# Tile 0 by expert id, six of W2's experts on ScalarE and VectorE, and the seam between the two layers in a new order

## The chip, the cores and the metric

The kernel runs on one core of one Trainium2 chip. The metric is device time in microseconds of one launch; the median of three runs of the kernel before is 280.23 us (279.22 to 280.51). Lower is better.

## What is computed

Eight sequences of 512 rows of 256 numbers pass two layers. The first is an attention that keeps only row sums: `q` and `k` are projections with rotary position, `o = exp(q k / 16)` summed over the causal keys, and `x1 = layernorm(x + relu(o * fc1_w + fc1_b) @ fc2_w.T + fc2_b)`. The second is a mixture of twelve experts, of which the router keeps three for each row and each of three weightings:

```python
h = gelu(sum_e C1[:, e] * (x1 @ W1[e].T))        # C1: softmax over the three largest logits, 0 elsewhere
y = sum_e C2[:, e] * (h @ W2[e].T) + C3 @ b2
out = layernorm(x1 + y)
```

The kernel reads from its own counts (`route_count`, `route_ids`, `load_ids`) which experts any row of a group of four tiles has chosen, computes three by their ids, and repeats everything with all twelve if a count shows more than three in a group; the trace has no such repeat.

## The kernel before, in words

There are 32 tiles (`NT`) of 128 rows, in eight groups of four (`GT`). Every engine runs one list of instructions in order; all waits between engines are semaphores written out by hand, so the order inside each engine's list is the schedule.

**The first layer** goes in eight chunks c = 0 to 7 (`NCH`) of four sequences each. TensorE projects four column blocks (`project(c, 0..3)`, line 920) and takes the scores of the chunk before (`scores`, line 933). ScalarE copies each projection out of PSUM (`qk_copy`, line 661) and takes the exponentials (`exps`, line 669). VectorE turns by position (`rope`, lines 1289 and 1295). Between these, `early_aux(c, j, early)` places the steps of the second layer's groups 0 and 1 by a list `EARLY` (line 340): ScalarE's `normed(0, 0)` (line 713) stands in chunk 4 ahead of `w_high(0)`, `qk_copy(4, 2)` and `exps(3, 1)`; TensorE's `x1_transpose(0, 0)` (line 1007) and `gate_spread(3)` (line 943) stand at the end of chunk 4, ahead of `project(5, 0)`. `normed(g, 0)` waits for `rstd_done`, which GpSimd's `norm_scale(g)` (lines 496 to 499) raises; that one waits for VectorE's `norm_stats(g)` (lines 1365 and 1369).

**The weights** W1 and W2 are each scaled by a power of two and split into a high and a low half in 16 bits. Experts 0 to 3 (`NB = 4`) of each go to ScalarE (`w_high`, line 699) and VectorE (`w_low`, line 1334). The other eight of each go to GpSimd (`w_piece`, three instructions: line 468 scales into `wtmp`, line 470 rounds, line 471 subtracts), one after another; the first waits for the DMAs of `fc2s`, which read from `wtmp`. GpSimd's loop (lines 567 to 586) runs `norm_scale(0)` at (3, 3), ahead of all pieces, and `norm_scale(1)` before piece 5.

**The seam** is the stretch between the last projection and the steady loop (`for i in range(GT, NT + 2)`). TensorE's list for it stands in lines 1176 to 1235, VectorE's in 1580 to 1616, ScalarE's in 846 to 871, GpSimd's in 585 to 611. Tile 0 is computed there with all twelve experts of W1 (`first`) and of W2 (`second(0, ...)`), since the ids come late; tiles 1 to 3 take three experts by id (`routed_first`, `second`). A product of a tile with an expert is six matmuls (`products`, line 1117) into one of four PSUM banks (`place`, `before`); VectorE adds most of them (`add_slot`, line 1535), ScalarE the first one of a tile (`begin`, line 783). Tile t goes through `gelu` (line 788), `h_transpose` (line 1197), `h_high` (line 830), `h_low` (line 1575), and W2's products. PSUM bank `XPOSE` is shared by `x1_transpose` (copied out by `x1_high`, line 720, and `x1_low`, line 1377), `C3_transpose` and `gate_transpose` (line 955, copied by `gate_copy`, line 690); whoever writes it waits for the readers of the one before. Bank `ROWS` is shared by `fc` (line 995, read by `fc_add`, line 1359) and `bias` (line 1059, read by `bias_copy`, line 726).

**The loop** runs from i = 4. In i = 4 ScalarE does `normed(3, 0)`, `begin_second(2)`, `h_high(3)`, `bias_copy`, `begin(4)`, `exp_route(2)` (line 705), `gelu(4)`. Exp and gelu need different tables, and a table load stands in the trace where they alternate.

Of the kernel before, what the change touches and what calls it, by code (L numbers as in the profile page):

```python
# [33 lines left out]
NB = 4  # L34
# [51 lines left out]
def build(nc, x, xT, wqkT, gate, fc2, p_w, uT, w1T, w2T, b2e, constb, constf, out):  # L86
    ctx = ExitStack()
    with ctx:
# [142 lines left out]
        w_split = sem("w_split")  # L231
        wlo_done = sem("wlo_done")
# [71 lines left out]
        def experts_of(t):  # L304
            return NE if t == 0 else TOPK

# [22 lines left out]
        def dense_expert(m, j):  # L329

            return NB - 1 - j if m and j < NB else j

        def last(t, m):
            return t, m, experts_of(t) - 1
# [24 lines left out]

        PARTS = (slice(0, NB), slice(NB + 2, NB + 6), slice(NB + 6, WS))  # L360
        HALVES = [slice(p.start + 2 * n, p.start + 2 * n + 2) for p in PARTS for n in range(2)]

# [3 lines left out]
        def _(sp):  # L366
# [12 lines left out]
            def load_experts(m, w):  # L379
                sp.dma_start(Wf[:, WS * m:WS * m + NB, :], w[:, 0:NB, :]).then_inc(ld_w[m], 16)  # L380
                sp.dma_start(Wf[:, WS * m + NB + 2:WS * (m + 1), :], w[:, NB:NE, :]).then_inc(ld_w[m], 16)

# [48 lines left out]
        def _(pool):  # L431
# [101 lines left out]
            def select_of(g):  # L533
# [5 lines left out]
                t = slice(max(GT * g, 1), GT * (g + 1))  # L539
# [106 lines left out]
        def _(act):  # L646
# [47 lines left out]
            def w_high(n):  # L694
                m, e = n // NB, NB - 1 - n % NB
                act.wait_ge(scale_done, 1)
                if n % NB:
# [77 lines left out]
            def begin(t):  # L775
                n = slot[t, 0, 0]
                if t == 0:
                    act.wait_ge(C_done, 1)
                elif t % GT == 0 or t == 1:
                    act.wait_ge(csel_done, t // GT + 1)  # L780
                act.wait_ge(slot_done, n + 1)
                c0 = C[:, 0, 0, 1:2] if t == 0 else Csel[:, t, 0, 0:1]
                act.activation(acc1[:, t % 2, :], bank[place[n]][:, 0:DIM], ACT.Copy, scale=c0).then_inc(acc_begun, 1)
# [6 lines left out]
            for c in range(NCH):  # L790
# [4 lines left out]
                if c == 0:  # L795
                    act.wait_ge(ld_const, 16 * 6)
                if c:
                    exps(c - 1, 0)
                early_aux(c, 0, early)
                early_aux(c, 1, early)  # L800
                if c == 2:
                    w_sum(0)
# [5 lines left out]
                if c:  # L808
                    exps(c - 1, 1)
                if c == 2:  # L810
# [11 lines left out]
                if c == NCH - 2:  # L822
                    x1_high(1, 0)
                    w_high(NB)
                if c == NCH - 1:
                    w_high(NB + 1)
# [43 lines left out]
            begin(3)  # L870
            gelu(3)
# [41 lines left out]
        def _(pe):  # L913
# [114 lines left out]
            def route_count(g):  # L1028
# [3 lines left out]
                tiles = range(1 if g == 0 else 0, GT)  # L1032
                for t in tiles:
                    mm = pe.matmul(bank[MISC][0:1, Z:Z + NM * NE], const(C_ONES, 1),
                                   mask[:, NR * t:NR * t + NM, :].rearrange("p g e -> p (g e)"),
                                   start=(t == tiles[0]), stop=(t == GT - 1))
# [84 lines left out]
            def mixture(t, m, lhs, js):  # L1121
                for j in js:
# [4 lines left out]
                    e = dense_expert(m, j) + 1 if t == 0 else held_ids[t // GT][REC * m + j]  # L1127
                    products(bank[place[n]], lhs, m, e).then_inc(slot_done, 1)
# [13 lines left out]
            for c in range(NCH):  # L1142
# [12 lines left out]
                if c:  # L1155
                    scores(c - 1, 0)
                project(c, 2)
                early_aux(c, 2, early)
                if c == NCH - 1:
                    route_count(0)  # L1160
# [11 lines left out]

            def first(js):
                mixture(0, 0, lambda hx, c: x1T[:, 0, hx, c, :], js)

            x1_transpose(1, 1)
            pe.wait_ge(exp_done, SPC * (NCH - 1))
            pe.wait_ge(w_split, NE - NB)
            pe.wait_ge(wlo_done, NB)
            first(range(0, 2))  # L1180
            pe.wait_ge(qk_copied, 4 * NCH)
            first(range(2, 4))
            fc(2, 0)
            first(range(4, 6))
            pe.wait_ge(gate_copied, 4)
            load_ids(0)
            scores(NCH - 1, 0)
            first(range(6, 8))
            fc(2, 1)
            scores(NCH - 1, 1)  # L1190
            first(range(8, NE))
# [14 lines left out]

            C3_transpose(0)
            routed_first(1)
# [4 lines left out]
            pe.wait_ge(wlo_done, NM * NB - 1)  # L1213
            second(0, range(0, NB - 1))
            pe.wait_ge(wlo_done, NM * NB)
            second(0, range(NB - 1, NB))
            pe.wait_ge(w_split, NM * (NE - NB) - 2)
            second(0, range(NB, NB + 2))
            bias(0, 1)
            second(0, range(NB + 2, NE - 2))  # L1220
            x1_transpose(2, 0)
            pe.wait_ge(w_split, NM * (NE - NB))
            second(0, range(NE - 2, NE))
            h_transpose(1)
            routed_first(2)
            fc(3, 0)
            gate_transpose(2)
            route_count(1)
            second(1, range(0, 1))
            fc(3, 1)  # L1230
            second(1, range(1, TOPK))
            h_transpose(2)
            x1_transpose(2, 1)
            routed_first(3)
# [38 lines left out]
        def _(dve):  # L1273
# [57 lines left out]
            def w_low(n):  # L1331
                m, e = n // NB, NB - 1 - n % NB
# [63 lines left out]
            def route_strike(g, halves=(0, 1)):  # L1396
# [5 lines left out]
                for n in range(n3 // 2 * halves[0], n3 // 2 * (halves[-1] + 1)):  # L1402
                    if g == 0 or n % NR == NM:
# [4 lines left out]
            def route_mask(g):  # L1408
                wait(dve, count_done, g)
                wait(dve, ezm_done, g)  # L1410
                if g == 0:
# [343 lines left out]
```

## Time and profile before

| | |
|---|---|
| median of 3 runs | 280.23 us |
| time of the profiled execution | 280.48 us |
| its span | 278.7 us |
| TensorE busy | 257.4 us (92%) |
| VectorE, GpSimd, ScalarE busy | 213.2, 180.2, 173.9 us |
| mean granted TensorE clock | 0.98 of full |

The profiled execution is one run; its time is 1.78 us above its span. PE is TensorE, DVE is VectorE, ACT is ScalarE, POOL is GpSimd. Starts are counted from the start of the span. An "idle before" names what ended the wait. Instructions of one engine overlap a little, so the time that one takes in a queue is the distance to the next start rather than its own duration.

### The profile page before, as it was taken

How to read it: one execution, taken by the hardware profiler on the slowest of the kernel's cores; microseconds unless marked ns; L12 is line 12 of the kernel's file. 1: busy time of each engine (PE TensorE's matmuls, PEld its weight loads, DVE VectorE, ACT ScalarE, POOL GpSimd, SP SyncE). 2: the span in 40 equal slices, each digit the busy share in tenths (PEclk: the TensorE clock that was granted, in tenths of full speed). 3: DMA queues.
4: the chain of work that ended last, by engine and by line, in shares of the span. 5: the costliest groups of instructions: out<-in, count | busy, mean ns of one | idle time of the engine just before them, and what ended most of it. 6: DMA issues, size and time to landing. Idle time of an engine off the chain costs nothing.

```text
span 278.7 us, 6485 instructions
## 1 busy us (share of the span) xinstructions
PE 257.4 (92%) x2016; PEld 191.4 (69%) x2016; DVE 213.2 (77%) x668; ACT 173.9 (62%) x376; POOL 180.2 (65%) x367
## 2 busy tenths in 40 slices
PE   7999999998989985998999999999999999899980
PEld 5445444554436773877789798799798798798960
DVE  0359959859969865688998899899897788766671
ACT  2235975765852730675958957967878858656541
POOL 2640004999989899747885775775775864856551
PEclk9999999999999996899999999999999999999996
DMA  7999994996000000000010101001011010111012
GB/s 226 378 397 372 164 221 72 220 151 84 0 1 2 0 4 0 0 5 17 13 31 22 34 24 39 22 20 42 19 26 35 20 40 19 33 32 38 23 36 61
DMA packets 19546, 20.51 MB, mean 74 GB/s; under 512 B 1643, under 2 KB 18870, under 8 KB 18998
## 3 DMA queue, kind: packets, MB, share of 16 engines
q1 hardware_dynamic: 18518, 19.14, 27.9%
q10 hardware_dynamic: 992, 0.93, 1.2%
q8 instruction: 18, 0.29, 0.4%
q14 instruction: 18, 0.15, 0.2%
HBM read 15.78 MB, written 4.19 MB: 72 GB/s over the span
## 4 chain that ended last, share of the span: by engine, by line
PE 37%; POOL 21%; SPq 16%; ACT 12%; issue 6%; DVE 5%; DMA 1%; POOLq 0%; ACTq 0%; DVEq 0%
PE bank L1117 31%; POOL W L471 7%; POOL wtmp L468 5%; POOL W L470 5%; SPq L371 4%; SPq L376 3%; ACT L705 3%; SPq L393 2%; SPq L380 2%; DVE early L1535 2%; ACT early L726 2%; PE bank L1197 2%; ACT L788 2%; SPq L404 1%; PE bank L995 1%
## 5 line engine op out<-in xcount | busy, mean ns | idle before, releaser
L1117 PE MATMUL bank<-W,early 128*128 (+1 forms) x630 | 77.7, 278 | 6.0 <-DVE early L1535 3.7
L1117 PE MATMUL bank<-W,x1T 128*128 (+1 forms) x630 | 75.9, 273 | 0.5 <-ACT early L837 0.5
L1117 PEld LDWEIGHTS bank<-W,early 128*128 128x128 f16 x630 | 61.9, 100 | 15.8 <-issue 4.2
L1117 PEld LDWEIGHTS bank<-W,x1T 128*128 128x128 f16 x630 | 60.9, 98 | 8.6 <-issue 1.1
L920 PE MATMUL bank<-early,wqk 128*128 128x512 f32 x128 | 60.1, 602 | 1.1 <-DMA early<-in_xT 1.1
L1535 DVE SCALAR_TENSOR_TENSOR early<-bank,Csel,early 128x256 f32<-128x256 f32 x95 | 45.7, 481 | 9.2 <-PE bank L1117 2.7
L591 POOL TENSOR_TENSOR early<-early 128x256 f32<-128x256 f32 x29 | 21.0, 725 | 28.4 <-DVE early L1535 27.1
L920 PEld LDWEIGHTS bank<-early,wqk 128*128 128x128 f32 x128 | 22.4, 190 | 21.8 <-issue 21.2
L661 ACT ACTIVATE qk<-bank 128x512 bf16<-128x512 f32 x32 | 19.0, 595 | 29.1 <-PE bank L920 28.9
L788 ACT ACTIVATE early<-early 128x256 f32<-128x256 f32 x32 | 13.3, 417 | 35.5 <-DVE early L1535 35.4
L1289 DVE TENSOR_TENSOR xturn<-qk,turn 128x2048 bf16<-128x2048 bf16 x16 | 20.4, 1276 | 15.7 <-ACT qk L661 15.7
L713 ACT ACTIVATE x<-xs,shift,rstd 128x256 f32<-128x256 f32 x32 | 17.4, 593 | 9.4 <-POOL shift L499 9.4
L843 ACT ACTIVATE early<-early,shift,rstd 128x256 f32<-128x256 f32 x32 | 18.8, 587 | 4.5 <-POOL shift L599 4.4
L471 POOL TENSOR_TENSOR W<-wtmp,W 128x512 f16<-128x512 f32 x16 | 20.6, 1289 | 1.4
L1535 DVE SCALAR_TENSOR_TENSOR early<-bank,Csel,xs 128x256 f32<-128x256 f32 x31 | 14.7, 473 | 8.4 <-PE bank L1117 7.2
L496 POOL TENSOR_SCALAR ve<-mv 128x4 f32<-128x4 f32 x8 | 2.8, 352 | 28.0 <-DVE mv L1369 27.5
L669 ACT ACTIVATE expd<-bank 128x128 bf16<-128x128 f32 (+3 forms) x32 | 13.6, 435 | 10.9 <-PE bank L935 10.8
L504 POOL TENSOR_TENSOR xs<-early,x 128x512 f32<-128x512 f32 x16 | 20.3, 1267 | 0.0
L598 POOL TENSOR_TENSOR rstd<-ve,minus_half 128x1 f32<-128x1 f32 x32 | 18.0, 561 | 2.7
L830 ACT ACTIVATE early<-bank,ipow 128x256 f16<-128x256 f32 x32 | 14.9, 467 | 5.4 <-PE bank L1197 5.2
L1575 DVE SCALAR_TENSOR_TENSOR early<-bank,ipow,early 128x256 f16<-128x256 f32 x32 | 14.7, 460 | 3.8 <-ACT early L830 3.8
L468 POOL TENSOR_SCALAR wtmp<-W,scale 128x512 f32<-128x512 f32 x16 | 15.4, 960 | 0.9 <-DMA fc2s<-wtmp 0.9
(139 smaller groups left out, 451.6 us busy)
## 6 DMA issues: line engine op xcount, KB each, us to landing
early<-in_xT SPq DMA_DIRECT2D x16, 256.0 KB, 7.8
xs<-in_x SPq DMA_DIRECT2D x32, 128.0 KB, 6.8
out<-early SPq DMA_DIRECT2D x32, 128.0 KB
W<-in_w1T SPq DMA_DIRECT2D x1, 2048.0 KB, 12.2
W<-in_w2T SPq DMA_DIRECT2D x1, 2048.0 KB, 12.8
W<-in_w1T SPq DMA_DIRECT2D x1, 1024.0 KB, 7.7
W<-in_w2T SPq DMA_DIRECT2D x1, 1024.0 KB, 14.3
wqk<-in_wqkT ACTq DMA_DIRECT2D x1, 512.0 KB, 3.8
```

The costliest lines, as they stand in the source:

```text
L468: link(pool.tensor_scalar(wtmp[:, n % 2, :], Wf[:, WS * m + e + 2, :], scale[:, 1 + m:2 + m], 0.0, ALU.mult, ALU.add))
L471: pool.tensor_tensor(W[:, m, e + 1, 1, :], wtmp[:, n % 2, :], W[:, m, e + 1, 0, :], ALU.subtract)\
L504: pool.tensor_tensor(xs[:, t:t + 2, :].rearrange("p t d -> p (t d)"), brows[:, h, :], x1[:, g % 3, 2 * h:2 * h + 2, :].rearrange("p t d -> ...
L591: pool.tensor_tensor(y[:, t % 4, :], y[:, t % 4, :], part[:, t % 2, :], ALU.add).then_inc(late_added, 1)
L598: link(pool.tensor_tensor(rstd2[:, p:p + 1], ve2[:, p:p + 1], minus_half[:, 0:1], ALU.pow))
L661: act.activation(qk[:, c % 2, g, :, :].rearrange("p s n -> p (s n)"), bank[PROJ[n % 2]][:, :], ACT.Copy)\
L788: act.activation(hact[:, t % 2, :], acc1[:, t % 2, :], ACT.Gelu).then_inc(gelu_done, 1)
L843: act.activation(y[:, t % 4, :], y[:, t % 4, :], ACT.Identity, bias=shift2[:, p:p + 1], scale=rstd2[:, p:p + 1]).then_inc(y_done, 1)
L920: mm = pe.matmul(bank[PROJ[n % 2]][:, :], wqk[:, k, g, :], xTb[:, c % 4, k, :, :].rearrange("p s n -> p (s n)"), start=(k == 0), stop=(k = ...
L1117: mm = pe.matmul(where[:, 0:DIM], lhs(hx, c), w, start=(k == 0), stop=(k == 5))
L1289: link(dve.tensor_tensor(xturn[:, :, :, :, :], src, turns, ALU.mult))
L1535: dve.scalar_tensor_tensor(sums, bank[place[n]][:, 0:DIM], c, before, ALU.mult, ALU.add)\
```

## The change

Tile 0 takes the three experts of its group's ids, as all other tiles do, for W1 and for W2; `dense_expert` and the twelve-expert lists go. `NB` becomes a pair: four experts of W1 and six of W2 are split by ScalarE and VectorE. GpSimd's last six (of W2) are scaled in place by ScalarE (`w_pre`), and GpSimd rounds and subtracts only. `load_ids(0)` moves ahead of the seam, and the seam's lists are in a new order on all four engines: three tiles and then the fourth of W1's products come before tile 0's of W2. In chunk 7, `route_count(0)` moves ahead of `project(7, 2)`, `rope(7, 1)` is run in the loop, `w_pre(8)` to `w_pre(10)` and `w_low(4)` are added. `begin(t)` also waits for `gelu_done`. `route_mask(0)` takes the form of the other groups, with four strikes in place of twelve. The diff, cut to its core (removed lines of the seam's lists that only moved are left out with their context):

```diff
-NB = 4
+NB = (4, 6)
+HERE, THERE = NB[0], NE - NB[0]
...
-        def experts_of(t):
-            return NE if t == 0 else TOPK
...
-            order = [(i - 2, 1, j) for j in range(experts_of(i - 2))] if i >= 2 else []
-            order += [(i, 0, j) for j in range(experts_of(i))] if i < NT else []
+            seconds = () if i < GT else (0, 1, 2) if i == GT else (i - 2,)
+            order = [(t, 1, j) for t in seconds for j in range(TOPK)]
+            order += [(i, 0, j) for j in range(TOPK)] if i < NT else []
...
+        def here(n):
+            return (0, NB[0] - 1 - n) if n < HERE else (1, NB[1] - 1 - (n - HERE))
+
+        def there(n):
+            return (0, NB[0] + n) if n < THERE else (1, NB[1] + n - THERE)
...
             def w_piece(n):
-                m, e = n // (NE - NB), NB + n % (NE - NB)
+                m, e = there(n)
                 if n == 0:
                     pool.wait_ge(fc2_spread, 16 * NP)
                     pool.wait_ge(scale_done, 1)
+                if m:
+                    raw = Wf[:, WS * m + e + 2, :]
+                    pool.wait_ge(pre_done, n - THERE + 1)
+                    pool.wait_ge(w_split, n)
+                    link(pool.tensor_copy(W[:, m, e + 1, 0, :], raw))
+                    pool.tensor_tensor(W[:, m, e + 1, 1, :], raw, W[:, m, e + 1, 0, :], ALU.subtract).then_inc(w_split, 1)
+                    return
...
-            piece = 0
-            for c in range(NCH):
-                for j in range(4):
-                    if (c, j) == (NCH - 1, 1):
-                        continue
-                    if (c, j) == (3, 3):
-                        norm_scale(0)
-                    if (c, j) == (5, 1):
-                        norm_scale(1)
-                    if (c, j) == (6, 1):
-                        chosen_exps(0)
-                        weights_of(0)
-                    if (c, j) == (6, 2):
-                        C3_split(0)
-                        select_of(0)
-                    if c >= 4:
-                        w_piece(piece)
-                        piece += 1
-            bias_add(0, 0)
-            w_piece(piece)
+            for n in range(THERE):
+                if n == 3:
+                    norm_scale(0)
+                if n == 5:
+                    norm_scale(1)
+                w_piece(n)
+            chosen_exps(0)
+            weights_of(0)
+            select_of(0)
+            C3_split(0)
+            for n in range(THERE, 2 * NE - sum(NB)):
+                if n == 2 * NE - sum(NB) - 1:
+                    bias_add(0, 0)
+                w_piece(n)
...
             norm_scale(2)
+            bias_add(0, 1)
             gate_parts(2)
-            bias_add(0, 1)
+            chosen_exps(1)
             row_scale(0)
-            chosen_exps(1)
...
+            def w_pre(n):
+                m, e = there(n)
+                act.wait_ge(scale_done, 1)
+                raw = Wf[:, WS * m + e + 2, :]
+                act.activation(raw, raw, ACT.Copy, scale=scale[:, 1 + m:2 + m]).then_inc(pre_done, 1)
...
             begin(0)
+            w_pre(THERE + 3)
+            begin(1)
+            w_pre(THERE + 4)
+            w_pre(THERE + 5)
             exps(NCH - 1, 0)
-            w_high(NB + 2)
+            w_high(HERE + 2)
             exps(NCH - 1, 1)
-            w_high(NB + 3)
+            w_high(HERE + 3)
+            C3T_copy(0)
             gelu(0)
-            C3T_copy(0)
-            begin(1)
+            gelu(1)
+            begin(2)
+            w_high(HERE + 4)
+            bias_copy(0, 0)
             h_high(0)
-            bias_copy(0, 0)
-            gelu(1)
+            gelu(2)
+            w_high(HERE + 5)
+            begin(3)
+            h_high(1)
+            bias_copy(0, 1)
+            gelu(3)
             normed(2, 0)
-            bias_copy(0, 1)
+            exp_route(1)
             x1_high(2, 0)
-            exp_route(1)
             normed(2, 1)
-            h_high(1)
-            begin(2)
-            gelu(2)
-            gate_copy(2)
             final(0)
             h_high(2)
             x1_high(2, 1)
-            begin(3)
-            gelu(3)
+            gate_copy(2)
...
+            load_ids(0)
+            x1_transpose(1, 1)
+            pe.wait_ge(exp_done, SPC * (NCH - 1))
+            pe.wait_ge(w_split, THERE)
+            pe.wait_ge(wlo_done, HERE)
+            routed_first(0, range(0, 2))
+            pe.wait_ge(qk_copied, 4 * NCH)
+            routed_first(0, range(2, TOPK))
+            fc(2, 0)
+            routed_first(1, range(0, 2))
+            pe.wait_ge(gate_copied, 4)
+            scores(NCH - 1, 0)
+            routed_first(1, range(2, TOPK))
+            fc(2, 1)
+            scores(NCH - 1, 1)
             C3_transpose(0)
-            routed_first(1)
+            routed_first(2)
             pe.wait_ge(exp_done, SPC * NCH)
             h_transpose(0)
             bias(0, 0)
             route_logits(1)
...
+            h_transpose(1)
+            routed_first(3)
             bias(0, 1)
...
+            pe.wait_ge(wlo_done, sum(NB))
+            pe.wait_ge(w_split, 2 * NE - sum(NB))
+            second(0, range(TOPK))
             x1_transpose(2, 0)
...
             fc(3, 0)
...
+            second(1, range(TOPK))
             h_transpose(2)
             x1_transpose(2, 1)
-            routed_first(3)
+            route_count(1)
+            fc(3, 1)
+            gate_transpose(2)
             fc(4, 0)
...
+            first_mixture(0)
             fc_add(2, 0)
...
             x1_low(1, 1)
...
+            w_low(HERE + 1)
+            first_mixture(1)
             fc_add(2, 1)
...
+            w_low(HERE + 2)
             norm_stats(2)
...
+            w_low(HERE + 3)
+            first_mixture(2)
             h_low(0)
...
+            w_low(HERE + 4)
             route_max(1)
...
+            w_low(HERE + 5)
+            first_mixture(3)
+            h_low(1)
+            second_mixture(0)
+            x1_low(2, 0)
             route_strike(1)
...
+            route_mask(1)
             row_stats(0)
...
             fc_add(3, 0)
...
+            second_mixture(1)
             route_sums(1)
...
             row_stats(1)
             h_low(2)
             x1_low(2, 1)
...
+            route_ids(1)
+            fc_add(3, 1)
+            norm_stats(3)
             fc_add(4, 0)
```

## Rows read from the trace of the kernel before

**Rows 1.** The page: busy us, share of the span and instructions of each engine.
```profile
PE 257.4 (92%) x2016; PEld 191.4 (69%) x2016; DVE 213.2 (77%) x668; ACT 173.9 (62%) x376; POOL 180.2 (65%) x367
```

**Rows 2.** Timeline, GpSimd: start us, us, engine line operation, count, idle before.
```profile
44.30 1.12 POOL L496 TENSOR_SCALAR ve<-mv 128x4 f32<-128x4 f32 x1 [26.88 <-DVE mv L1369]
...
48.48 1.00 POOL L468 TENSOR_SCALAR wtmp<-W,scale 128x512 f32<-128x512 f32 x1 [0.91 <-DMA fc2s<-wtmp]
...
56.45 0.69 POOL L468 TENSOR_SCALAR wtmp<-W,scale 128x512 f32<-128x512 f32 x1
...
59.03 0.69 POOL L468 TENSOR_SCALAR wtmp<-W,scale 128x512 f32<-128x512 f32 x1
```

**Rows 3.** Timeline, ScalarE, in chunk 4.
```profile
47.78 1.09 ACT L713 ACTIVATE x<-xs,shift,rstd 128x256 f32<-128x256 f32 x2
...
50.21 0.40 ACT L669 ACTIVATE expd<-bank 128x256 bf16<-128x256 f32 x1
```

**Rows 4.** Timeline, TensorE, chunks 4 to 6.
```profile
51.02 0.60 PE L1007 MATMUL bank<-identf,x 128*128 128x128 f32 x4
51.46 0.60 PE L943 MATMUL bank<-identf,o 128*32 128x128 f32 x4
...
68.32 0.50 PE L933 MATMUL bank<-x1T,qr 128*128 128x384 bf16 x2 [0.83 <-DVE x1T L1295]
...
84.04 0.60 PE L1007 MATMUL bank<-identf,x 128*128 128x128 f32 x4
```

**Rows 5.** Windows: busy us of PE, PEld, DVE, ACT, POOL; granted PE clock; DMA.
```profile
106.00:107.00 1.00, 0.00 (x0) 0.00 (x0) 0.00 (x0) 0.00 (x0) 1.00 (x2) 0.98 0.00 0
107.00:108.00 1.00, 0.04 (x1) 0.07 (x2) 0.63 (x2) 0.00 (x0) 0.97 (x2) 0.50 0.00 0
...
113.00:114.00 1.00, 1.00 (x8) 0.73 (x6) 0.23 (x1) 0.50 (x2) 0.93 (x2) 0.60 0.00 0
```

**Rows 6.** Timeline, TensorE, in the seam.
```profile
97.51 2.13 PE L1117 MATMUL bank<-W,x1T 128*128 x18
...
107.96 2.72 PE L1117 MATMUL bank<-W,early 128*128 128x256 f16 x12 [3.66 <-DVE early L1535]
...
127.53 0.77 PE L1023 MATMUL bank<-MT,x1T 128*128 128x36 f16 x24 [0.29 <-DVE x1T L1377]
```

**Rows 7.** Timeline, GpSimd, in the seam.
```profile
98.63 0.61 POOL L470 CAST W<-wtmp 128x512 f16<-128x512 f32 x1
...
100.46 1.13 POOL L468 TENSOR_SCALAR wtmp<-W,scale 128x512 f32<-128x512 f32 x1
...
109.97 0.23 POOL L496 TENSOR_SCALAR ve<-mv 128x4 f32<-128x4 f32 x1
...
111.85 0.42 POOL L483 TENSOR_TENSOR hg<-o,gwb 128x136 f32<-128x136 f32 x1
...
115.68 1.27 POOL L504 TENSOR_TENSOR xs<-early,x 128x512 f32<-128x512 f32 x1
```

**Rows 8.** Timeline, VectorE, in the seam.
```profile
108.77 0.36 DVE L1385 TENSOR_SCALAR zs<-bank,iscale 128x144 f32<-128x144 f32 x1
...
110.58 1.52 DVE L1535 SCALAR_TENSOR_TENSOR early<-bank,C,early 128x256 f32<-128x256 f32 x3
...
119.58 0.68 DVE L1377 TENSOR_TENSOR x1T<-bank,x1T 128x512 f16<-128x512 f32 x1
...
128.17 0.25 DVE L1369 BATCH_NORM_AGGREGATE mv<-stats 128x2 f32<-128x6 f32 x2
```

**Rows 9.** Timeline, ScalarE, in the seam.
```profile
95.53 0.72 ACT L699 ACTIVATE W<-W,scale 128x512 f16<-128x512 f32 x1
96.27 1.28 ACT L788 ACT_TABLE_LOAD   x1
98.07 0.42 ACT L788 ACTIVATE early<-early 128x256 f32<-128x256 f32 x1 [0.52 <-DVE early L1535]
...
133.14 1.28 ACT L705 ACT_TABLE_LOAD   x1
```

More of the change, by code:

```diff
@@ L358, in later @@
             return 2 <= g < NG
-        PARTS = (slice(0, NB), slice(NB + 2, NB + 6), slice(NB + 6, WS))
-        HALVES = [slice(p.start + 2 * n, p.start + 2 * n + 2) for p in PARTS for n in range(2)]
+        PARTS = (slice(0, NB[0]), slice(NB[0] + 2, NB[0] + 6), slice(NB[0] + 6, WS))
+        HALVES = [slice(e + 2 * (e >= NB[1]), e + 2 * (e >= NB[1]) + 2) for e in range(0, NE, 2)]
         block = ctx.enter_context(nc.Block())
@@ L796, in _ @@
                     act.wait_ge(ld_const, 16 * 6)
+                if c == NCH - 1:
+                    w_pre(THERE)
                 if c:
@@ L800, in _ @@
                 early_aux(c, 1, early)
+                if c == NCH - 1:
+                    w_pre(THERE + 1)
                 if c == 2:
@@ L809, in _ @@
                     exps(c - 1, 1)
+                if c == NCH - 1:
+                    w_pre(THERE + 2)
                 if c == 2:
@@ L823, in _ @@
                     x1_high(1, 0)
-                    w_high(NB)
+                    w_high(HERE)
                 if c == NCH - 1:
-                    w_high(NB + 1)
+                    w_high(HERE + 1)
             def h_high(t):
@@ L1031, in route_count @@
                 begun["count"] += 1
-                tiles = range(1 if g == 0 else 0, GT)
-                for t in tiles:
+                for t in range(GT):
                     mm = pe.matmul(bank[MISC][0:1, Z:Z + NM * NE], const(C_ONES, 1),
                                    mask[:, NR * t:NR * t + NM, :].rearrange("p g e -> p (g e)"),
-                                   start=(t == tiles[0]), stop=(t == GT - 1))
+                                   start=(t == 0), stop=(t == GT - 1))
                 mm.then_inc(count_done, 1)
@@ L1126, in mixture @@
                         pe.wait_ge(acc_begun if act else slot_added, count)
[L1127 to L1128 removed]
+                    products(bank[place[n]], lhs, m, held_ids[t // GT][REC * m + j]).then_inc(slot_done, 1)
             def load_ids(g):
@@ L1156, in _ @@
                     scores(c - 1, 0)
+                if c == NCH - 1:
+                    route_count(0)
                 project(c, 2)
                 early_aux(c, 2, early)
-                if c == NCH - 1:
-                    route_count(0)
                 if c:
@@ L1171, in _ @@
                     gate_spread(c - 1)
[L1173 to L1191, printed above, removed]
             def h_transpose(t):
@@ L1458, in early @@
                         route_sums(k + 1)
-                        w_low(NB)
                         route_ids(k + 1)
@@ L1521, in _ @@
                 if c == NCH - 1:
-                    break
+                    w_low(HERE)
                 rope(c, 1)
@@ L1549, in first_mixture, with second_mixture @@
                     add_slot(t, 0, j, sums, sums)
-            def second_mixture(t, js=range(TOPK)):
+            def second_mixture(t):
                 sums = y[:, t % 4, :]
-                for j in js:
+                for j in range(TOPK):
                     if j == 0 and late(t):
@@ L1577, in h_low @@
                                          ALU.mult, ALU.subtract).then_inc(hlo_done, 1)
-            rope(NCH - 1, 1)
-            first_mixture(0, (1, 2, 3))
+            first_mixture(0)
             fc_add(2, 0)
-            first_mixture(0, (4,))
-            w_low(NB + 1)
-            first_mixture(0, (5,))
             x1_low(1, 1)
-            first_mixture(0, (6, 7))
-            w_low(NB + 2)
+            w_low(HERE + 1)
+            first_mixture(1)
             fc_add(2, 1)
-            first_mixture(0, range(8, NE))
+            w_low(HERE + 2)
             norm_stats(2)
-            w_low(NB + 3)
+            w_low(HERE + 3)
+            first_mixture(2)
             h_low(0)
-            first_mixture(1)
-            second_mixture(0, range(0, 3))
+            w_low(HERE + 4)
             route_max(1)
-            second_mixture(0, range(3, 8))
+            w_low(HERE + 5)
[3 more added lines that the diff above has]
+            x1_low(2, 0)
             route_strike(1)
-            second_mixture(0, range(8, NE))
+            route_mask(1)
             row_stats(0)
-            h_low(1)
-            x1_low(2, 0)
-            route_mask(1)
             fc_add(3, 0)
-            first_mixture(2)
+            second_mixture(1)
             route_sums(1)
-            route_ids(1)
-            norm_stats(3, (0,))
-            second_mixture(1)
-            fc_add(3, 1)
             row_stats(1)
@@ L1613, in _ @@
             x1_low(2, 1)
-            norm_stats(3, (1,))
-            first_mixture(3)
+            route_ids(1)
+            fc_add(3, 1)
+            norm_stats(3)
             fc_add(4, 0)
```

69 lines of the change are left out of this document (21 added, 48 removed).

## The prediction

> **What bounds the kernel now.** I read first the busy shares on the page: TensorE is busy for 92% of the span [rows 1], so time leaves the kernel only with TensorE's work or its gaps. The windows then say where it isn't full: one hole in the seam. The timeline of TensorE there shows 3.66 us without a matmul before 107.96 [rows 6]; the windows show the granted clock at half (1.2 instead of 2.4 GHz) from 106.96 (0.98 of that microsecond) to 113.8 (0.60 of the last one) [rows 5]. Between 107.96 and 113.8 TensorE worked at half speed: 5.84 / 2 = 2.9 us lost. The waits in that hole end in VectorE and behind it in GpSimd's pieces of W2. So the seam has 18 products to lose, plus a hole and a slow stretch. Then I read the three other engines' timelines in the places that the diff reorders, the early one too: GpSimd's list is rewritten from chunk 4 on.
>
> **Step 1, the early part: norm_scale(0) now stands behind three pieces.** Before, it starts at 44.30, and the first piece waits until 48.48 for a DMA [rows 2]. ScalarE's normed(0, 0), which needs it, starts at 47.78 with no wait [rows 3]. After, the first piece still starts at 48.48, and norm_scale(0) comes behind pieces 0, 1 and 2. A piece with VectorE idle takes 59.03 - 56.45 = 2.58 us [rows 2]; the first one, still beside VectorE's turn, I put at 3.2: 48.48 + 3.2 + 2 x 2.58 = 56.85. A norm_scale takes 111.85 - 109.97 = 1.88 [rows 7]: its result is there at 58.8. ScalarE runs its list in order, so normed(0, 0), w_high(0), qk_copy(4, 2) and exps(3, 1) start at 58.85 instead of 47.78, 11.1 late. TensorE is queued behind that: x1_transpose(0, 0), at 51.02 before, needs normed(0, 0) (58.85 + 1.09 = 59.95), and gate_spread(3), at 51.46 before [rows 4], needs the last exponential of exps(3, 1), which ends 0.4 to 0.5 after 50.21 [rows 3], so 50.7 + 11.1 = 61.8 after. **Stall: 61.8 - 51.46 = +10.3.** All of it is exposed, because VectorE (w_low(0), rope(4, 1)) waits for the same ScalarE instructions and TensorE's next projection stands behind the transposes. Bounds: 9.5 (all pieces at 2.58, less slack) to 11.3 (pieces at 3.2).
>
> TensorE is then idle for some 9 us, much more than the 3.66 us after which rows show half clock. I charge the same slow stretch, **+2.9**, between 1.7 (the clock rises while x1_transpose and gate_spread run) and 3.5.
>
> One thing comes back. GpSimd does pieces 3 and 4 while the others are late, and then waits for norm_stats(1); VectorE runs rope(5, 0) and w_low(2) without it beside, and the wait of 0.83 before 68.32 [rows 4] goes: **-0.8** (0 to -0.8). From there to the seam everything is shifted together. Below I count seam times as before's, without the shift.
>
> **Step 2, chunk 7.** GpSimd is free at 79.2, so chosen_exps(0) starts when the mask is there. route_count(0) ahead of project(7, 2) makes TensorE wait about 0.2 for the mask; load_ids(0) ahead of x1_transpose(1, 1) costs some 0.35 of issue. +0.5 together: x1_transpose(1, 1), at 84.04 before [rows 4], starts at 84.6. The three w_pre and w_low(4) lie in ScalarE's and VectorE's waits for projections: 0. The ids and weights of tile 0 (C, then six copies) are ready by 84.5, before ScalarE's begin(0) at 85.6: 0, up to +1.5 if GpSimd is slowed.
>
> **Step 3, the seam.** Removed: 9 + 9 products of six matmuls and their 18 additions. 18 matmuls take 2.13 at most, 1.96 from start to start [rows 6]: 0.65 a product, 11.8 for 18. On VectorE an addition is 1.52 / 3 = 0.5 [rows 8]: 9 us less. Added on VectorE and ScalarE: two more halves of W2 each (0.7 each [rows 9]) and six w_pre on ScalarE. GpSimd loses two pieces (5.2) and six scalings.
> What ends last there is no longer TensorE's work but a chain, which I follow.
> (a) TensorE from 84.6: transpose 0.44, six products 3.9, two fc 2.1, the two halves of the last scores 2.0: 93.1.
> (b) ScalarE: exps(7, 1) to 93.8, w_high(7) 0.7, C3T_copy 0.5, table load 1.28 [rows 9], gelu(0) and gelu(1) 0.7, begin(2) 0.45, w_high(8) 0.6, bias_copy 0.5, h_high(0) 0.45: 99.0. TensorE has done routed_first(2) at 95.3 and waits for this.
> (c) VectorE: h_low(0) 0.4, w_low(8) 0.65, route_max(1) 110.58 - 108.77 = 1.8 [rows 8], w_low(9) 0.65, two additions of tile 3: 103.5. GpSimd's last piece: 85.9 + five at 1.83 (100.46 - 98.63 [rows 7]) and contention is 96; it then waits for bias_copy(0, 0) (98.6), bias_add 1.25, a piece 1.83: 101.7, under the 102.6 at which w_low(9) lets tile 0's second products start. So GpSimd isn't last, by 0.9.
> (d) ScalarE: gelu(3) 0.4, normed(2, 0) 1.05, table load and exp 1.6, x1_high(2, 0) 0.5: 107.1.
> (e) VectorE from x1_low(2, 0) to the end of norm_stats(3): before 119.58 to 128.42, 8.84 [rows 8]; without routed_first(2)'s two additions (-1.0), with the strikes (+0.6) and row_stats(0) (+0.6), and contention: 9.3. It ends at 116.4. gate_parts(2), 115.68 - 111.85 = 3.8 [rows 7], ends at 108.8 and is just hidden.
> Before, it ended at 128.42: -12.0. In i = 4 no table load stands before exp_route(2) any more, since no gelu comes between the two exps: 1.28 [rows 9], of which 0.4 counts, for VectorE is 11.7 to 12 ahead only. Eight hand-offs between engines that I counted at nothing give 0.4 back. **Seam: -12.0**, between -10 and -15: TensorE's own list, with its waits at 95.3, 97.8 and 111.2, would stand 11.8 ahead at route_logits(2), 127.53 before [rows 6].
>
> The load in (b) was hidden before (it ran at 96.27, and ScalarE then waited 0.52 for VectorE, until 98.07) and is now on the path. It ends at 97.55 and the row after it shows no further halt beyond that wait [rows 9]; I take 1.28. The Trainium skill, ScalarE: Activation LUTs, What ACT_TABLE_LOAD costs, gives each switch of table 1.38 us of drain more, 2.66 in all; by it the chain would be 1.4 longer and the time 282.1.
>
> **Sum**, against the profiled execution's 280.48: +10.3 + 2.9 - 0.8 - 12.0 = +0.4, 280.9. The median of the runs is 0.25 lower, so the forecast is **280.7**: no change that can be measured (about 0.5%, 1.4 us, is what a measurement of this kernel can tell from nothing). The steady loop and the end stay as they are: 0.
>
> **Rivals.**
> *A second slow stretch of the clock, in the seam* (the side that is slower). TensorE waits 1.4 and 1.7 us between 95.3 and 99.5, and 0.8 and 2.6 us with little work between 109.3 and 113.9. For it: the clock fell in a hole of 3.66. Against: no single hole is that long. It decides if these waits together bring half clock as that one did. It costs up to 2.9, of which the other engines' chain hides a third: +1.5 to +2.9, 282.7. 0.28.
> *The seam is TensorE's own.* If the handovers in (b) to (e) overlap better, the ceiling is 11.8 of products, 3.66 of hole and 2.9 of slow clock, less 0.5: -17.8, 275.1; half way -15, 277.7. Against: VectorE and ScalarE stand in strict order with route_max(1) and two halves of W2 between. 0.14.
> *The stall isn't there*: an instruction ahead of norm_scale(0) that I misread. Then -12.4: 268. All in the diff speaks against. 0.03.
> *GpSimd ends last*: its pieces at 2.5 beside VectorE instead of 1.83 make the last one 3 us later, 283 to 285. 0.05.
>
> **How the numbers follow.** The forecast has 0.50; its terms' bounds give it 278 to 283. Faster than 278.8: 0.08 of it, with 0.12 of the second rival and 0.03 of the third, 0.23. Slower than 281.6: 0.10 of it, 0.22 of the first, 0.05 of the last, 0.37. The same: 0.40. The range 277.4 to 284.4 leaves out about 0.1 on either side.
>
> **What would show it.** GpSimd's line 497 for group 0 at about 57 to 59 instead of 45; ScalarE idle before its first line 713 for some 11 us, ended by GpSimd; TensorE without matmuls from 51 to 60, then granted 0.5 for some 6 us; the first route_count 10 to 13 us late. In the seam: no hole of more than 2.7 us, a table load right behind C3T_copy, the end of norm_stats(3) 32 to 33 us after x1_transpose(1, 1) (44.4 before), and one exp in i = 4 without a load. Wrong if line 713 starts by 50, if the clock falls twice, or if tile 0's second products wait for GpSimd.

## The result: 1277.7 us, because the second layer runs twice

| kernel | median us | ratio to before, 95% interval |
|---|---|---|
| before | 280.37 (4 runs) | |
| changed | 1277.72 (1277.22 to 1278.04) | 4.560 [4.547, 4.574] |

The forecast was 280.7. Of all launches told of here one, of e5_bias_add_early, ran at a granted clock of 0.75, took 337.64 us and stays out of its ratio. The page of the changed kernel: its span, the busy time of each engine, the span in 40 slices of 31.9 us, the costliest groups, and one row of the DMA issues.

```profile
span 1276.2 us, 23884 instructions
...
PE 859.9 (67%) x6579; PEld 649.9 (51%) x6581; DVE 725.0 (57%) x2205; ACT 224.0 (18%) x478; POOL 201.7 (16%) x451
...
PE   9697999950000001788788788788788788788785
...
PEclk9899999985555555989898898898898898898898
...
L1138 PE MATMUL bank<-W,x1T 128*128 128x256 f16 (+1 forms) x2880 | 353.1, 275 | 257.2 <-DVEq L1655 231.0
L1670 DVE SCALAR_TENSOR_TENSOR early<-bank,C,early 128x256 f32<-128x256 f32 x704 | 340.7, 484 | 213.3 <-PE bank L1138 143.9
...
L1138 PE MATMUL bank<-W,early 128*128 128x256 f16 (+1 forms) x2880 | 385.1, 302 | 45.1 <-DVE early L1681 43.7
...
L1269 PE MATMUL bank<-identf,early 128*128 128x128 f32 x64 | 17.6, 366 | 83.2 <-ACT early L921 83.2
L942 PE MATMUL bank<-early,wqk 128*128 128x512 f32 x128 | 61.9, 617 | 0.3 <-DMA early<-in_xT 0.3
...
L1652 DVE TENSOR_SCALAR dz<-dz,esum,cscale 128x12 f32<-128x12 f32 x64 | 18.7, 292 | 9.6 <-DVE esum L1651 6.3
...
out<-early SPq DMA_DIRECT2D x64, 128.0 KB
```

The kernel before has TensorE busy for 257.4 us [rows 1], and the table ahead gives its span as 278.7. Here TensorE's row in slices is busy up to slice 9 (287 us), then come six slices (287 to 479 us) without a matmul, one with a little, then 24 slices (from 510.5 us) that look alike. 2880 matmuls for each of W1 and W2 are 32 tiles x 90: 72 of the 90 are twelve experts of six matmuls, 18 are the three by id. The output goes out in 64 DMAs instead of 32. So first the whole kernel ran by id, and then all 32 tiles again with all twelve experts. Only the second layer is repeated, though the description ahead says everything: the page counts 128 projections of the first layer (line 942), as before.

The place where it turns, in VectorE's timeline (start us, us, engine, line, operation, idle before):

```profile
274.68 0.14 DVE L1625 TENSOR_REDUCE over<-idf 1x1 f32<-1x16 f32 x1
274.85 0.14 DVE L1626 CAST overi<-over 1x1 int32<-1x1 f32 x1
279.69 0.17 DVE L1644 COPY dz<-C 128x12 f32 x1 [4.70 <-DMA out<-early]
```

Lines 1625 and 1626 reduce the fourth id of each group to one number and write it where the engines read it. In the kernel before they end VectorE's list, at 272.92 and 273.09, followed by nothing. Here line 1644, the first of the branch `If(some != 0)`, begins at 279.69, after the last store. The windows of the two parts behind it (columns as in [rows 5]):

```profile
280.00:504.00 224.00, 0.00 (x0) 0.00 (x0) 113.60 (x703) 0.00 (x0) 0.00 (x0) 0.50 0.00 0
...
510.00:1270.00 760.00, 604.96 (x4639) 461.89 (x4636) 404.42 (x859) 47.06 (x95) 32.54 (x93) 0.90 0.02 5
```

From 279.69 to 504.07 only VectorE works: it takes the three largest of each row's twelve weights again, 64 passes (32 tiles, W1 and W2) of ten dependent instructions on 128x12 numbers, 224.4 / 64 = 3.5 us a pass. From there to 1276.2 it is 772 us for 32 tiles, 24.1 us each, with the granted clock at 0.90 of full. Together the repeat costs 1276.2 - 276.7 = 999.5 us, counted from the end of the routed part (ScalarE's last normalisation of the routed part starts at 276.12 and takes 0.60).

The routed part alone is what I had predicted, and it ends 1.76 us later than before (274.68 against 272.92). Its parts are compared below.

### The profile page after: what moved, and what is told of

It reads as the page before. It is cut to its first block, busy times and chain, and to the rows that moved or that the text cites. A ratio compares the mean times of both kernels' runs of the same rounds, so it can differ in the third digit from the quotient of the medians.

```text
span 1276.2 us, 23884 instructions
## 1 busy us (share of the span) xinstructions
PE 859.9 (67%) x6579; PEld 649.9 (51%) x6581; DVE 725.0 (57%) x2205; ACT 224.0 (18%) x478; POOL 201.7 (16%) x451
## 4 chain that ended last, share of the span: by engine, by line
PE 41%; DVE 30%; issue 15%; ACT 5%; DVEq 5%; SPq 1%; POOL 1%; DMA 1%; ACTq 0%; POOLq 0%
PE bank L1138 33%; DVE early L1670 17%; PE bank L942 3%; DVEq L1670 2%; DVE dz L1652 2%; PE bank L1269 1%; DVE early L1681 1%; DVE zrest L1647 1%; ACT early L924 1%; DVE early L1677 1%; ACT early L921 1%; DVEq L1642 1%; DVE top L1645 1%; DVE C L1654 1%; DVE dz L1644 1%
## 5 line engine op out<-in xcount | busy, mean ns | idle before, releaser
L1138 PE MATMUL bank<-W,x1T 128*128 128x256 f16 (+1 forms) x2880 | 353.1, 275 | 257.2 <-DVEq L1655 231.0
L1670 DVE SCALAR_TENSOR_TENSOR early<-bank,C,early 128x256 f32<-128x256 f32 x704 | 340.7, 484 | 213.3 <-PE bank L1138 143.9
L1138 PEld LDWEIGHTS bank<-W,x1T 128*128 (+1 forms) x2880 | 262.3, 98 | 336.4 <-issue 231.6
L1138 PE MATMUL bank<-W,early 128*128 128x256 f16 (+1 forms) x2880 | 385.1, 302 | 45.1 <-DVE early L1681 43.7
L1138 PEld LDWEIGHTS bank<-W,early 128*128 128x128 f16 x2880 | 309.0, 108 | 116.8 <-issue 53.8
L1269 PE MATMUL bank<-identf,early 128*128 128x128 f32 x64 | 17.6, 366 | 83.2 <-ACT early L921 83.2
L1673 DVE SCALAR_TENSOR_TENSOR early<-bank,C,xs 128x256 f32<-128x256 f32 x32 | 15.5, 484 | 57.6 <-PE bank L1138 57.6
L1644 DVE COPY dz<-C 128x12 f32 x64 | 11.1, 173 | 28.7 <-DVE C L1654 24.0
L1677 DVE TENSOR_SCALAR early<-bank,C 128x256 f32<-128x256 f32 x32 | 15.5, 484 | 19.0 <-PE bank L1138 19.0
L1652 DVE TENSOR_SCALAR dz<-dz,esum,cscale 128x12 f32<-128x12 f32 x64 | 18.7, 292 | 9.6 <-DVE esum L1651 6.3
L1534 DVE SCALAR_TENSOR_TENSOR early<-bank,Csel,xs 128x256 f32<-128x256 f32 x32 | 15.1, 473 | 10.3 <-PE bank L1138 9.0
```

Of the source, the lines that this page charges most:

```text
L1138: mm = pe.matmul(where[:, 0:DIM], lhs(hx, c), w, start=(k == 0), stop=(k == 5))
L1269: tr = pe.transpose(bank[HT][:, c * P:(c + 1) * P], hact[:, 0, c * P:(c + 1) * P], identf[:, :])
L1534: dve.scalar_tensor_tensor(sums, bank[place[n]][:, 0:DIM], Csel[:, t, m, j:j + 1], before, ALU.mult, ALU.add)\
L1644: link_kept(dve.tensor_copy(dz[:, 0, :], weights), 1)
L1652: link_kept(dve.tensor_scalar(dz[:, 0, :], dz[:, 0, :], esum[:, 0, 0:1], cscale[:, m:m + 1], ALU.mult, ALU.mult), 9)
L1670: dve.scalar_tensor_tensor(sums, bank[e % RING][:, 0:DIM], c, sums, ALU.mult, ALU.add)\
```

## Why the repeat runs, and six experiments

**Theory.** Tile 0's rows choose more than three experts between them. The kernel before computed tile 0 with all twelve and left it out of `route_count(0)` (`tiles = range(1 if g == 0 else 0, GT)`, line 1032); the change computes it by id and counts it, so the count shows a fourth expert and sets off the repeat. **Rivals**: the new form of `route_mask(0)` or the in-place scaling breaks a count; or tile 0 is within three, and something else is slow.

The reference's formulas, evaluated on its inputs, say how many different experts the 128 rows of each tile choose:

```
tile        0   1   2   3 ... 31
C1 (W1)    12   3   3   3      3
C2 (W2)    11   3   3   3      3
C1 by position, tile 0's 16 and the next two (8 rows each):
9 8 7 6 8 6 6 6 4 3 3 3 3 3 3 3 | 3 3
```

Tile 0 holds the first 16 positions of the eight sequences. There the causal sum has few terms; from position 9 on (10 for C2), the eight rows of a position choose three experts. This is the reference's arithmetic and no run; the two runs that follow test it on the chip.

**e1_skip_tile0_in_count.** The changed kernel with tile 0 left out of the count again. It leaves out, for tile 0, every expert outside the three of its group.

```diff
-                for t in range(GT):
+                for t in range(1 if g == 0 else 0, GT):
...
-                                   start=(t == 0), stop=(t == GT - 1))
+                                   start=(t == (1 if g == 0 else 0)), stop=(t == GT - 1))
```

> The changed kernel, but route_count(0) leaves tile 0 out again, as before; tile 0 is still computed with the three experts of its group's ids, so its rows lose their other experts. Theory (the repeat is set off by tile 0's rows alone, which choose more than three experts between them): no repeat, and the time is that of the routed part of the changed kernel, whose last ScalarE instruction ends at 276.7 against 275.0 before: 280.2 + 1.8 = 282.0, between 281.3 and 282.8. Rival A (the new form of route_mask(0), a comparison with the third value in place of strikes, or the in-place scaling of W2 breaks a count): the repeat still runs, about 1277. Rival B (the slow part is the seam itself): far above 282 without a repeat.

Measured: 283.42 us, ratio 1.014 [1.010, 1.019]. No repeat. The new mask and the in-place scaling are in this kernel, so rival A is out, and so is B. The median is 0.6 above the stated range, which ended at 282.8. The profiled run of it has a span of 281.1, 2.4 more than before's. The surplus over the changed kernel's routed part (VectorE's line 1625 starts at 275.30 instead of 274.68) isn't from chunk 4: x1_transpose(1, 1) starts at 95.16, earlier than the 95.89 there. It arises behind that. There the granted clock is at half from 110.0 to 116.8 and from 127.0 to 133.9; in the changed kernel these stretches are 111.9 to 115.4 and 125.6 to 132.4. That they make the difference is likely and not shown by a run.

**e3_before_count_all.** The kernel before, tile 0 still with all twelve experts, but counted.

```diff
-                tiles = range(1 if g == 0 else 0, GT)
+                tiles = range(0, GT)
```

> The kernel before with one edit: route_count(0) counts tile 0 too (tiles = range(0, GT)). Nothing is left out. Theory (tile 0's rows choose more than three experts between them): the repeat with all twelve experts runs and the time is 280.2 + about 999.5, the distance from the end of the routed part to the end in the changed kernel's trace (1276.2 - 276.7): 1280, between 1277 and 1283. Rival (tile 0 is within three experts and something else of the change set the repeat off): 280.

Measured: 1282.23 us (two runs), ratio 4.58. VectorE's timeline of it at the same place:

```profile
271.89 0.14 DVE L1635 TENSOR_REDUCE over<-idf 1x1 f32<-1x16 f32 x1
...
276.90 0.17 DVE L1654 COPY dz<-C 128x12 f32 x1 [4.70 <-DMA out<-early]
```

One number in one loop turns 280 into 1282, with nothing else of the change. Together with the run before, this shows the cause from both sides: counting tile 0 is enough, and not counting it takes the repeat away.

**e4_before_scale_late.** The early stall by itself: the kernel before with `norm_scale(0)` behind three pieces.

```diff
-                    if (c, j) == (3, 3):
+                    if (c, j) == (4, 3):
                         norm_scale(0)
```

> The kernel before with norm_scale(0) moved behind GpSimd's pieces 0, 1 and 2, where the change has it; nothing else. Theory of the prediction: TensorE is idle from 51 to about 60.5, then at half clock to about 66: 10.3 to 11 of stall, 2.9 of slow clock, less up to 0.8: 280.2 + 12 = 292, between 290.5 and 294. Rival (VectorE and GpSimd get ahead during the stall and give some of it back, above all the hole of 3.66 us and the slow clock in the seam, since GpSimd's pieces come early): 285 to 290.

Measured: 291.03 us, ratio 1.042 [1.036, 1.048]: +10.8. TensorE's timeline in chunk 4, at the start of the seam and in it:

```profile
60.57 1.12 PE L1007 MATMUL bank<-identf,x 128*128 128x128 f32 x4 [9.29 <-ACT x L713]
62.39 1.04 PE L943 MATMUL bank<-identf,o 128*32 128x128 f32 x4 [0.70 <-ACT expd L669]
...
95.56 0.60 PE L1007 MATMUL bank<-identf,x 128*128 128x128 f32 x4
...
119.49 1.88 PE L1117 MATMUL bank<-W,early 128*128 128x256 f16 x12 [3.66 <-DVE early L1535]
```

and the windows (columns as in [rows 5]):

```profile
54.00:55.00 1.00, 0.00 (x0) 0.00 (x0) 0.00 (x0) 0.00 (x0) 1.00 (x2) 1.00 1.14 130
55.00:56.00 1.00, 0.00 (x0) 0.00 (x0) 0.00 (x0) 0.00 (x0) 0.94 (x2) 0.78 1.16 131
...
65.00:66.00 1.00, 1.00 (x3) 0.26 (x1) 0.17 (x1) 0.96 (x2) 1.00 (x1) 0.60 1.16 131
66.00:67.00 1.00, 1.00 (x4) 0.63 (x4) 0.75 (x1) 0.58 (x1) 0.19 (x1) 1.00 1.14 130
```

gate_spread(3) starts at 62.39 instead of 51.46 [rows 4]: 10.9 of stall. The clock is at half from 55.6 to 65.8, the last 3.4 us of it under work, so the slow clock costs 1.7 here. x1_transpose(1, 1) is 11.5 late (95.56 against 84.04). The rival is right in one small thing: the end is only 10.4 late (span 289.1 against 278.7). The hole in the seam is still 3.66 us (119.49), but the slow stretch behind it falls later and shorter than in [rows 5]: from 120.4 to 123.8, 3.4 us under work instead of 5.84.

**e2_skip_and_scale_first.** The changed kernel without the stall: as e1, and `norm_scale(0)` first. It leaves out the same experts of tile 0.

```diff
+            norm_scale(0)
             for n in range(THERE):
-                if n == 3:
-                    norm_scale(0)
```

> As e1, and norm_scale(0) ahead of all pieces of GpSimd again. Theory of the stall in chunk 4 (TensorE idle 9.5 + 0.7 us there and then at half clock until about 66 us): all of the shift of 11.85 us that x1_transpose(1, 1) has in the changed kernel goes, its start is back at 84.0 to 84.6, and the time is 282.0 - 11.9 = 270, between 269 and 271.5. Rival (part of the shift comes from w_pre, w_low(4) and route_count in chunk 7, or the stall was cover for GpSimd's pieces, which then end last in the seam): 273 to 277.

Measured: 270.60 us, ratio 0.966 [0.963, 0.968]. The start of x1_transpose(1, 1) is back at 83.78. One position in GpSimd's list is worth 283.42 - 270.60 = 12.8 us. What the 18 products, their additions, the new split of the weights and the new order bring together is 280.22 - 270.60 = 9.6 us; but this kernel does less than the reference asks for.

**e5_bias_add_early.** Can the kernel before be had faster with all of its work? Its hole in the seam ends in `bias_add(0, 0)`, so that one alone was moved, to before piece 13.

```diff
                     if c >= 4:
+                        if piece == 13:
+                            bias_add(0, 0)
                         w_piece(piece)
                         piece += 1
-            bias_add(0, 0)
             w_piece(piece)
```

> The kernel before with GpSimd's bias_add(0, 0) ahead of its piece 13 instead of behind piece 14; nothing left out, tile 0 with all twelve experts. Reading of before's hole: TensorE waits from 104.3 to 107.96 for PSUM slots, VectorE (idle 5.00 until 107.33) for xs, which bias_add(0, 0) writes at 106.04 to 107.3 behind two pieces; bias_copied is there at 100.85. Theory: the hole of 3.66 and the 2.9 us of slow clock behind it go for the most part: 280.2 - 5.5 = 274.7, between 273 and 277. Rival (the wait only moves: pieces 14 and 15, 1.3 us later each, then hold tile 0's last W2 products): 278 to 280.

Measured: 280.65 us, ratio 1.003 [1.001, 1.006]. The theory fell: nothing is gained over the kernel before (279.82 beside it). The time is 0.65 above the rival's 278 to 280, and it comes by a wait that I hadn't named. TensorE, then ScalarE, in the seam:

```profile
113.48 1.11 PE L1008 MATMUL bank<-identf,x 128*128 128x128 f32 x4 [3.99 <-ACT x L714]
```

```profile
112.34 1.09 ACT L714 ACTIVATE x<-xs,shift,rstd 128x256 f32<-128x256 f32 x2 [9.19 <-POOL shift L499]
```

The wait of 3.66 is gone, and one of 3.99 stands before x1_transpose(2, 0), which needs normed(2, 0), which needs norm_scale(2), which stands behind GpSimd's last piece. The clock falls in it again (columns as in [rows 5]):

```profile
112.00:113.00 1.00, 0.00 (x0) 0.00 (x0) 0.00 (x0) 0.66 (x2) 0.84 (x4) 0.82 0.00 0
113.00:114.00 1.00, 0.52 (x3) 0.52 (x4) 0.00 (x0) 0.91 (x2) 0.89 (x2) 0.50 0.00 0
```

**e6_dense_six_here.** So GpSimd's whole chain has to end earlier. The kernel before, old order, all twelve experts for tile 0, with the change's split of the weights: `NB = (4, 6)`, `w_pre`, two instructions a piece. With two pieces fewer in all than before, the loop stops one short, so that `bias_add(0, 0)` still stands ahead of the last.

```diff
-NB = 4
+NB = (4, 6)
...
+                if m:
+                    raw = Wf[:, WS * m + e + 2, :]
+                    pool.wait_ge(pre_done, n - THERE + 1)
+                    pool.wait_ge(w_split, n)
+                    link(pool.tensor_copy(W[:, m, e + 1, 0, :], raw))
+                    pool.tensor_tensor(W[:, m, e + 1, 1, :], raw, W[:, m, e + 1, 0, :], ALU.subtract).then_inc(w_split, 1)
+                    return
...
-                    if c >= 4:
+                    if c >= 4 and piece < 2 * NE - sum(NB) - 1:
                         w_piece(piece)
                         piece += 1
             bias_add(0, 0)
             w_piece(piece)
...
             begin(0)
+            w_pre(THERE + 3)
+            w_pre(THERE + 4)
+            w_pre(THERE + 5)
...
             bias_copy(0, 0)
+            w_high(HERE + 4)
             gelu(1)
+            w_high(HERE + 5)
...
             first_mixture(1)
+            w_low(HERE + 4)
             second_mixture(0, range(0, 3))
+            w_low(HERE + 5)
```

> The kernel before, tile 0 with all twelve experts and nothing left out, old order of the seam, with the change's split alone: six of W2's experts on ScalarE and VectorE, the other six scaled in place by ScalarE and rounded and subtracted by GpSimd, bias_add(0, 0) ahead of GpSimd's last piece. Moving bias_add alone only moved the hole, from VectorE's wait to TensorE's wait for norm_scale(2), which stands behind GpSimd's last piece. Theory (GpSimd's chain of pieces, bias_add, norm_scale(2) is what holds the seam): two pieces of 2.6 and six scalings of 0.75 less end it some 6 us earlier, the hole and the slow clock behind it go, 280.2 - 6.5 = 273.7, between 272.5 and 276. Rival (VectorE's additions and two more low halves become the bound): 277 to 280.

Measured: 274.56 us, ratio 0.979 [0.977, 0.982], faster than both kernels, with nothing left out. Its longest waits of TensorE in the seam, and a window of that stretch:

```profile
104.90 0.83 PE L1150 MATMUL bank<-W,early 128*128 128x256 f16 x6 [0.64 <-DVE W L1367]
...
107.10 2.14 PE L1150 MATMUL bank<-W,early 128*128 128x256 f16 x18 [0.49 <-DVE early L1568]
```

```profile
104.00:106.00 2.00, 1.36 (x13) 0.99 (x11) 1.97 (x15) 0.00 (x0) 1.83 (x3) 1.00 0.00 0
106.00:108.00 2.00, 1.50 (x15) 1.11 (x13) 1.81 (x7) 1.26 (x3) 1.66 (x6) 1.00 0.00 0
```

GpSimd's last piece ends at 104.3 (before, 109.9), the waits are 0.64 and 0.49, and the granted clock stays full. The split alone thus brings 6.0 of the 9.6 us of the run e2_skip_and_scale_first, with all 18 products kept. If the two add up, which no run shows, the products, their additions and the new order together are worth some 3.6.

## Why the prediction was wrong, and where it held

**The step that failed** is in the sum: "The steady loop and the end stay as they are: 0." The end has a branch, and the change flips it. Behind it stands a sentence of step 3 that I costed and didn't question: "Removed: 9 + 9 products". I took tile 0's twelve experts for a matter of time (I wrote ahead that the ids come late). They were there because tile 0 needs them: twelve and eleven. The whole diff had the sign for it, in lines that the excerpt ahead leaves out: `route_count(0)` began at tile 1, and the change makes it begin at 0. I put route_count among the moved steps and gave its move a cost of 0.2 us; I read neither its range nor where its result goes, `ids`, `over`, `some != 0`. The description of the kernel ahead says that the repeat exists, and the profile of before can't price it, since no row of it lies in that branch. None of the rivals had it.

**What the rest came to.** Taken alone, the routed part was forecast at +0.4 against the profiled execution. It is +1.76 in the changed kernel's trace, and 283.42 against 280.22 in e1_skip_tile0_in_count. That +1.76 lies so near to +0.4 is partly luck: up to x1_transpose(1, 1) the changed kernel is 1.0 less behind than forecast, and from there to the end of norm_stats(3) it gains 1.7 less.

*Step 1, the stall.* ScalarE's and TensorE's rows in chunk 4 of the changed kernel:

```profile
59.48 1.09 ACT L725 ACTIVATE x<-xs,shift,rstd 128x256 f32<-128x256 f32 x2 [11.65 <-POOL shift L511]
```

```profile
60.62 1.12 PE L1029 MATMUL bank<-identf,x 128*128 128x128 f32 x4 [9.51 <-ACT x L725]
62.43 1.04 PE L965 MATMUL bank<-identf,o 128*32 128x128 f32 x4 [0.70 <-ACT expd L675]
```

Forecast: ScalarE at 58.85, gate_spread at 61.8, +10.3. Measured 59.48 and 62.43, +10.97. The 0.6 is a sum of two: the DMA that the first piece waits for let it start at 49.63 instead of 48.48 (+1.15), and the three pieces took 7.86 (49.63 to 57.49) where 3.2 + 2 x 2.58 = 8.36 was forecast (-0.5). The clock:

```profile
53.00:54.00 1.00, 0.00 (x0) 0.00 (x0) 0.00 (x0) 0.00 (x0) 0.92 (x2) 0.96 1.20 320
...
67.00:68.00 1.00, 1.00 (x4) 0.76 (x4) 0.00 (x0) 0.52 (x1) 0.00 (x0) 0.72 0.66 106
```

It is at half from 53.9 to 67.6, of which 5.1 under steady work: 2.6, forecast 2.9. x1_transpose(1, 1) starts at 95.89 instead of 84.04: +11.85, forecast +10.3 + 2.9 - 0.8 + 0.5 = 12.9. The wait of 0.83 [rows 4] is gone, as forecast, and of the 0.85 before the next chunk's scores 0.40 is left. Step 2's +0.5 isn't there: from x1_transpose(1, 0) to x1_transpose(1, 1) TensorE takes 95.89 - 85.86 = 10.03 us, before 84.04 - 73.39 = 10.65.

*Step 3, the seam.* The same landmarks in the changed kernel, TensorE:

```profile
95.89 0.60 PE L1029 MATMUL bank<-identf,x 128*128 128x128 f32 x4
...
109.11 0.41 PE L1197 MATMUL bank<-identf,early 128*128 128x128 f32 x2 [2.22 <-ACT early L799]
...
111.75 0.50 PE L1197 MATMUL bank<-identf,early 128*128 128x128 f32 x2 [1.42 <-DVE early L1572]
112.05 3.74 PE L1138 MATMUL bank<-W,x1T 128*128 x18
...
123.27 1.10 PE L1017 MATMUL bank<-fc2w,hgf 32*128 32x256 f32 x4 [0.66 <-DVE xs L1366]
126.59 1.06 PE L977 MATMUL bank<-cb,hgp 128*102 128x128 bf16 x8 [2.23 <-issue]
128.81 0.59 PE L1017 MATMUL bank<-fc2s,hgT 102*128 102x256 bf16 x2 [1.16 <-ACT hgT L696]
129.19 0.93 PE L1045 MATMUL bank<-MT,x1T 128*128 128x36 f16 x24
```

and the end of norm_stats(3) on VectorE:

```profile
129.12 0.38 DVE L1376 BATCH_NORM_AGGREGATE mv<-stats 128x2 f32<-128x6 f32 x4
```

From x1_transpose(1, 1) to there it is 129.50 - 95.89 = 33.6 us; before, 44.4. The gain is 10.8. The forecast of 12.0 has the 0.5 of step 2 in it, so from x1_transpose(1, 1) on it is 12.5, and 1.7 of it didn't come. The chain was the right one: the wait of 2.22 ends in ScalarE's gelu(0), the 1.42 in VectorE's h_low(0), and gate_transpose(2) begins right behind x1_low(2, 1), which ends at 126.49, after a wait of 2.23 (forecast 1.4, 1.7 and 2.6; the row names no engine, the list does). GpSimd's pieces were not last: its sixth ended at 114.3, and TensorE began tile 0's second products at 115.85 without a wait.

What was mis-sized stands in (b) to (d). By the prediction's steps gelu(0) begins at 93.8 + 0.7 + 0.5 + 1.28 = 96.3, 11.7 us behind x1_transpose(1, 1); measured is 108.55 - 95.89 = 12.7, with a wait of 0.52 in it, for VectorE's half of a weight, that (b) doesn't have. From there to x1_low(2, 0) it is 107.1 - 96.3 = 10.8 by the prediction and 120.08 - 108.55 = 11.5 in the trace; tile 3's 18 matmuls of W1 lie in it, at half clock: 3.74 us instead of 2.13 [rows 6]. The last part, (e), came out: 129.50 - 120.08 = 9.4, forecast 9.3.

At the end of norm_stats(3) the changed kernel is 129.50 - 128.42 = 1.08 behind, and at VectorE's last line 1.76. The 0.7 between them falls into the steady loop, which the sum has at 0; the half clock of the seam reaches into it, to 132.4, but no run isolates that.

*The first rival*, a second slow stretch, came, and twice (columns as in [rows 5]):

```profile
112.00:114.00 2.00, 2.00 (x12) 1.35 (x10) 1.89 (x15) 1.15 (x3) 1.92 (x3) 0.50 0.00 0
...
115.00:116.00 1.00, 1.00 (x10) 0.82 (x8) 0.64 (x3) 0.00 (x0) 1.00 (x1) 0.82 0.00 0
125.00:126.00 1.00, 0.00 (x0) 0.00 (x0) 0.97 (x5) 0.43 (x1) 0.79 (x3) 0.80 0.04 10
...
132.00:133.00 1.00, 1.00 (x9) 0.80 (x8) 0.05 (x1) 0.94 (x2) 0.85 (x3) 0.79 0.00 0
```

Half clock from about 111.9 to 115.4 and from 125.6 to 132.4. I had given it 0.28, arguing that no single hole is as long as the 3.66 of before. The first time it comes 0.2 us behind two holes of 2.22 and 1.42 with 1.2 us of work between; the second time inside the hole of 2.23 (124.36 to 126.59), which stands behind one of 0.66 and 1.1 us of work, and before the hole of 1.16. "The clock falls twice" stood among the prediction's own signs of being wrong. What it costs to the end wasn't taken apart by a run.

*The table load in the path.* ScalarE, changed kernel:

```profile
106.03 0.72 ACT L705 ACTIVATE W<-W,scale 128x512 f16<-128x512 f32 x1 [0.52 <-DVE W L1341]
106.66 0.57 ACT L743 ACTIVATE C3T<-bank 72x512 bf16<-72x512 bf16 x1
107.25 1.28 ACT L799 ACT_TABLE_LOAD   x1
108.55 0.72 ACT L799 ACTIVATE early<-early 128x256 f32<-128x256 f32 x2
```

The copy before it ends at 107.23, the load starts at 107.25 and ends at 108.53, and gelu starts at 108.55. The Trainium skill, ScalarE: Activation LUTs, What ACT_TABLE_LOAD costs, has 1.38 us of drain besides; the trace has room for 0.04. The 1.28 that I took was right, and the alternative of 282.1 rested on nothing that these rows show. The exp of i = 4 came without a load, as forecast.

## What to carry to other kernels

If a change takes away work that looks redundant, ask first what made its author put it there, and look at the data: which rows need it, and what in the kernel checks for the opposite. A branch that never runs in the profile of before has no row and no price, and belongs into the prediction as a rival whenever the change touches its condition. In an in-order engine a small instruction behind three long ones is at least as dear as they are (12.8 us here for one position in GpSimd's list, behind three pieces of 7.9 in all), and the hole here went only when the whole chain behind it ended earlier: moving the instruction that ended the wait brought nothing, lightening the engine brought 6 us.

## What the runs showed of the hardware that I had not expected

The start of the half clock after a long hole is not the same from run to run of nearly the same list. In chunk 4 the last matmul before the hole ended at 51.1 in the changed kernel and at 51.3 in e4_before_scale_late; the half clock came at 53.9 and at 55.6, and it ended at 67.6 and 65.8. The work lost was 2.6 and 1.7 us.

Holes of at most 2.25 us brought half clock like one of 3.66, and again not at one place. With a hole of 2.22 to 2.25 and one of 1.42 behind it, it came 0.2 us behind the second hole in the changed kernel, and 0.3 us into it (110.0) in e1_skip_tile0_in_count. At the hole of 2.23 of gate_transpose(2) it came inside in the changed kernel, and 0.7 us behind its end, at 115.9, in e2_skip_and_scale_first. The windows show it as a granted clock of 0.99 in 109 to 110 us and 0.50 behind in e1, and of 0.95 in 115 to 116 us and 0.50 behind in e2.

In the repeat the granted clock swings too: 0.90 on average over 760 us, with TensorE busy for 605 of them and 83.2 us of waits for gelu (2.6 a tile) before the transposes of line 1269.
